# An expert layer and a Mamba scan on one core: LayerNorm moved to the odd body, B copies ahead of evacuations, the last sums side by side, the fourth B product and SiLU one tile later

## The reference

```python
# L0: mixture of experts on every pixel (E = 4 experts, 192 hidden, the best 2 by router)
gates = softmax over the top 2 of (tokens @ router_w.T + router_b), 0 for the others
out   = sum_e gates[e] * (gelu(tokens @ fc1_w[e].T + fc1_b[e]) @ fc2_w[e].T + fc2_b[e])
x     = x + scale * out
# L1: Mamba over the pixels of each image, once forwards and once backwards
x_norm = (x - mean) * rsqrt(var + 1e-5) * gamma + beta          # over the 96 channels
xr, z  = split(x_norm @ W_in)                                   # 192 + 192
xr     = silu(causal_conv4(xr) + conv_b)
dt     = softplus((xr @ W_xproj[:, :6]) @ W_dt + b_dt);  Bm, Cm = xr @ W_xproj[:, 6:]
h_t    = exp(dt_t * A) * h_{t-1} + (dt_t * xr_t) * B_t          # 192 channels x 16 states
y      = (sum over the 16 states of h_t * C_t + xr * D) * silu(z)
out    = 0.5 * (y_forward + y_backward) @ W_out + x
```

## Time and profile before

| | |
|---|---|
| median of three runs | 6058.42 us |
| the profiled execution | 6065.3 us, of which span 6063.5 us |
| TensorE matmul busy | 4967.7 us (82%) |
| VectorE busy | 5276.6 us (87%) |
| ScalarE busy | 4307.0 us (71%) |
| GpSimd busy | 5156.9 us (85%) |
| mean granted TensorE clock | 0.855 of 2.4 GHz |
| DMA | 159 GB/s over the span |

### The profile page before, as it was taken

One profiled execution on the slowest core, in us unless ns is written; L12 is line 12 of the kernel. 1 busy time (PEld: TensorE's weight loads), 2 busy tenths in 40 slices (PEclk: granted clock), 3 DMA queues, 4 the chain that ended last, 5 costly groups with the idle time before them and its releaser, 6 DMA issues.

```text
span 6063.5 us, 68824 instructions
## 1 busy us (share of the span) xinstructions
PE 4967.7 (82%) x14273; PEld 1536.1 (25%) x14273; DVE 5276.6 (87%) x4474; ACT 4307.0 (71%) x6471; POOL 5156.9 (85%) x2127
## 2 busy tenths in 40 slices
PE   7777888878888888888888778887888888888787
PEld 7222222222222222222222222222222222222222
DVE  1239989998999989999899999999899998999998
ACT  0447777777777777777777777777677777777776
POOL 0039989998899998999898998989899998999898
PEclk9878789888888888887898789878888888988898
DMA  3046767676676767676776767666676767766776
GB/s 94 22 98 163 168 164 175 160 174 157 166 173 156 176 155 175 166 171 160 169 173 159 171 160 173 166 163 169 159 175 163 171 161 171 170 165 165 170 172 149
DMA packets 428356, 964.98 MB, mean 159 GB/s; under 512 B 58080, under 2 KB 58329, under 8 KB 394984
## 3 DMA queue, kind: packets, MB, share of 16 engines
q1 hardware_dynamic: 428008, 961.31, 65.6%
HBM read 776.98 MB, written 184.11 MB: 159 GB/s over the span
## 4 chain that ended last, share of the span: by engine, by line
issue 25%; PE 25%; DVE 14%; DMA 10%; POOL 9%; ACT 7%; SPq 2%; DVEq 1%; ACTq 0%; POOLq 0%
DVE X L1163 11%; PE ps L677 8%; POOL X L1250 4%; DMA bc_d<-bc 3%; PE ps L708 3%; POOL X L1240 3%; DMA lo_d<-bc 3%; DMA lo<-lo_d 2%; PE ps L699 2%; PE ps L702 2%; PE ps L656 2%; ACT ps L939 1%; DVE X L1147 1%; PE ps L717 1%; DMA y_d<-yf 1%
## 5 line engine op out<-in xcount | busy, mean ns | idle before, releaser
L1250 POOL TENSOR_TENSOR X<-X,cR 128x2048 f32<-128x2048 f32 x768 | 3479.1, 4530 | 62.0
L1163 DVE TENSOR_TENSOR_SCAN X<-ps,carry,X 128x512 f32<-128x512 f32 x2688 | 3261.6, 1266 | 87.9 <-ACT ps L939 71.3
L939 ACT ACTIVATE ps<-hi,amat 128x512 f32<-128x512 f32 x2048 | 1377.1, 684 | 829.3 <-DVE X L1163 826.1
L1147 DVE TENSOR_TENSOR X<-hi,ps 128x2048 f32<-128x2048 f32 x512 | 1164.6, 2275 | 244.6 <-PE ps L708 133.7
L1240 POOL TENSOR_TENSOR X<-lo,bR 128x2048 f32<-128x2048 f32 x258 | 1168.5, 4529 | 21.8 <-DMA lo<-lo_d 21.8
L708 PE MATMUL ps<-X,red 128*32 128x512 f32 x6144 | 922.9, 676 | 305.6 <-POOL X L1250 304.5
L677 PE MATMUL ps<-win,w_u 97*128 97x512 f32 (+1 forms) x2080 | 1112.7, 684 | 5.9 <-DMA win<-xn_d 4.8
L939 ACT ACTIVATE ps<-lo,amat 128x512 f32<-128x512 f32 x1026 | 688.8, 679 | 163.1 <-DVE X L1163 120.7
L692 PE MATMUL ps<-xr,wd 128*96 128x512 f32 (+1 forms) x520 | 381.6, 826 | 280.4 <-ACT xr L894 227.3
L640 PE MATMUL ps<-xp,w 96*128 96x512 f32 x864 | 524.2, 738 | 54.8 <-DMA xp<-in_x 51.2
L677 PEld LDWEIGHTS ps<-win,w_u 97*128 97x128 f32 (+1 forms) x2080 | 369.7, 188 | 669.5 <-issue 634.5
(11 more groups left out here) (111 smaller groups left out, 4352.1 us busy)
## 6 DMA issues: line engine op xcount, KB each, us to landing
hi<-hi_d SPq DMA_DIRECT2D x516, 512.0 KB, 8.2
bR<-bc_d SPq DMA_DIRECT2D x516, 256.0 KB, 4.6
lo<-lo_d SPq DMA_DIRECT2D x516, 256.0 KB, 4.5
cR<-bc_d SPq DMA_DIRECT2D x516, 256.0 KB, 7.1
hi_d<-S SPq DMA_DIRECT2D x258, 256.0 KB, 8.0
y_d<-yf SPq DMA_DIRECT2D x128, 256.0 KB, 8.8
yb<-y_d SPq DMA_DIRECT2D x128, 256.0 KB, 7.4
win<-xn_d SPq DMA_DIRECT2D x130, 196.3 KB
```

The source lines that it names most:

```text
L939: A_(p_a[i % RING][:, :], dt, ACT.Exp, scale=amat[:, column(i):column(i) + 1]).then_inc(s_exp, 1)
L1147: V.tensor_tensor(X[:, slot(par, s), :, :], hi[:, par, HIGH:2 * HIGH, :], p_b[:, :].unsqueeze(1).to_broadcast([P, BATCH, CH]), ALU.mult).t ...
L1163: V.tensor_tensor_scan(h, a, h, 0.0 if head else carry[:, i:i + 1], ALU.mult, ALU.add).then_inc(s_scan, 1)
L1250: G.tensor_tensor(batch(par, s), batch(par, s), quads(cR, par, s), ALU.mult).then_inc(s_hc, 1)
```

## The change

LayerNorm leaves the even body for the odd one. `ln_mean` heads the odd body's list on TensorE (where `hidden(3)` stood; this goes behind `hidden(5)`), `ln_var` stands behind the last two sums and ahead of `y_begin(1)`; `ln_centred` moves on ScalarE to i = 5, behind the evacuation, `ln_rstd` to i = 8, behind the copy of the output; `normalise` on GpSimd to between the second and the third C product; `store_xn` on SP to the odd body. The operations themselves stay as they are.

On ScalarE in every body, `copy_b` 0 goes from i = 5, behind `evacuate`, to i = 4, and `copy_b` 1 from behind `copy_out` to ahead of it. On TensorE the sums of batches 4 and 5 of the body before stand together behind the third expert product in even bodies, with the other three behind them, and the sum of batch 2 stands ahead of `project(1)` and no longer behind it. The fourth B product on VectorE and SiLU on ScalarE move from i = 19 to i = 20. The bank lists follow.

```diff
--- before.py
+++ after.py
@@ -100,9 +100,9 @@
     out = [("OUT", 1)] if fin else []
     z = [("Z1", 2), ("Z0", 1)] if next_rev else []
     if odd:
-        return (D_BANKS + [("H3", 0)] + out + [("H4", 2), ("H5", 1), ("G3", 2), ("G4", 0), ("U0", 1), ("G5", 2), ("U1", 0)] + z)
-    return (D_BANKS + [("Y2", 0), ("MU", 0)] + out + [("GT", 2), ("VAR", 0), ("H0", 1), ("H1", 2), ("H2", 0),
-                                                       ("G0", 2), ("G1", 0), ("U0", 1), ("G2", 2), ("U1", 0)] + z)
+        return (D_BANKS + [("MU", 0), ("VAR", 0)] + out + [("H4", 2), ("H5", 1), ("H3", 0), ("G3", 2), ("G4", 0), ("U0", 1), ("G5", 2), ("U1", 0)] + z)
+    return (D_BANKS + [("Y2", 0)] + out + [("GT", 2), ("H0", 1), ("H1", 2), ("H2", 0),
+                                           ("G0", 2), ("G1", 0), ("U0", 1), ("G2", 2), ("U1", 0)] + z)
 
 
 def count(uses, bank):
@@ -568,7 +568,7 @@
                 load_high(n + 1, nxt)
                 if fin:
                     store_out(*finished(img, q, rev, odd)[:2], u)
-                if not odd:
+                if odd:
                     store_xn(*piece_before(img, j), pc - 1)
                 if not rev:
                     store_y(1, n, chunk_of(q, rev, odd))
@@ -768,7 +768,7 @@
                 windows = (img * (BODIES // 2) + q + ((NCH // 2) * rev + 2)) * 16
 
                 if odd:
-                    hidden(3, pc, u)
+                    ln_mean(u)
                     sum_states(n - 1, NB - 2, nxt)
                     sum_states(n - 1, NB - 1, nxt)
                 else:
@@ -778,24 +778,22 @@
                         expert_out(m, u, None)
                     if before is not None:
                         sum_states(n - 1, NB - 2, nxt)
-                    expert_out(3, u, None)
-                    expert_out(4, u, None)
-                    if before is not None:
                         sum_states(n - 1, NB - 1, nxt)
-                    expert_out(5, u, None)
+                    for m in range(3, HT):
+                        expert_out(m, u, None)
                     expert_bias(u)
+                if odd:
+                    ln_var(pc - 1, u)
                 y_begin(1, n, f, par)
-                if not odd:
-                    ln_mean(u)
                 if fin:
                     finish(u, n - 1, finished(img, q, rev, odd)[2], nxt)
                 sum_states(n, 0, par)
                 if odd:
                     hidden(4, pc, u)
                     hidden(5, pc, u)
+                    hidden(3, pc, u)
                 else:
                     gates_transposed(nimg, j, u)
-                    ln_var(pc - 1, u)
                     for m in range(3):
                         hidden(m, pc, u)
                 sum_states(n, 1, par)
@@ -806,8 +804,8 @@
                 project(0, par, urev, u)
                 gate_rows(rows + 2, u, even)
                 y_begin(0, n, f, par)
+                sum_states(n, 2, par)
                 project(1, par, urev, u)
-                sum_states(n, 2, par)
                 if nrev:
                     project_z(1, nxt, u)
                     project_z(0, nxt, u)
@@ -984,21 +982,21 @@
                         softplus_start(0, u, n + 1)
                     if i == 3:
                         softplus_log(0, n + 1)
+                    if i == 4:
+                        copy_b(n, 0, par)
                     if i == 5 and before == 0:
                         evacuate(n - 1, 0, img * NCH + (NCH - 1 if rev else q * 2 + odd - 1))
-                    if i == 5:
-                        copy_b(n, 0, par)
                     if i == 6 and not odd:
                         copy_x2(u, pc - 1)
-                    if i == 7 and not odd:
+                    if i == 5 and odd:
                         ln_centred(u, pc - 1)
                     if i == 8:
+                        copy_b(n, 1, par)
                         if before == 1:
                             copy_out(u)
-                        copy_b(n, 1, par)
                     if i == 9 and not odd:
                         copy_gates(u)
-                    if i == 10 and not odd:
+                    if i == 8 and odd:
                         ln_rstd(u, pc - 1)
                     if i == 11:
                         gelu(u, range(3, 6) if odd else range(3))
@@ -1008,7 +1006,7 @@
                         evacuate(n, 1, img * NCH + q * 2 + odd)
                     if i == 16:
                         copy_b(n, 3, par)
-                    if i == 19:
+                    if i == 20:
                         silu_x(u, par)
                         if nrev:
                             silu_z(u, nxt)
@@ -1192,8 +1190,8 @@
                         gate_y(n, True, par)
                     if i in (14, 15, 16):
                         gate_hidden((3 if odd else 0) + i - 14, u)
-                    if i in (7, 11, 15, 19):
-                        times_b(n, i // 4 - 1, par)
+                    if i in (7, 11, 15, 20):
+                        times_b(n, (7, 11, 15, 20).index(i), par)
                     scan(n, i, rev, par, head)
 
             bodies(dve, body)
@@ -1265,10 +1263,10 @@
                 times_c(n, 0, par, rev)
                 times_x(0, u, nxt)
                 times_c(n, 1, par, rev)
+                if odd:
+                    normalise(pc - 1)
                 times_c(n, 2, par, rev)
                 times_b(n + 1, 0, nxt)
-                if not odd:
-                    normalise(pc - 1)
                 times_c(n, 3, par, rev)
                 times_b(n + 1, 1, nxt)
                 times_c(n, 4, par, rev)
```

## The result

The changed kernel takes 6233.97 us (median; 6225.16 to 6243.95), the kernel before, run beside it, 6061.58 (6050.98 to 6075.53): a ratio of 1.029, with a 95% interval of 1.0273 to 1.0306. It is 2.9% slower. The prediction of 6005 us and its range up to 6090 are both wrong. The profiled execution took 6225.16 us, of which span 6223.3, with a mean granted clock of 0.841 (before 0.855).

The account below looks back on a forecast made before the run. VectorE and GpSimd were taken to bound the kernel, with VectorE's idle time to win. Terms: -108 - 74 + 19 + 14 - 12 - 10 + 80 + 38 = -53 us off the 6058.42 median, giving 6005 us; range 5900 to 6090.

Parts of the forecast that it names:

- last sums side by side: TensorE, reverse even body: gated output waits less for the last sum; 0.5 x 24 bodies = -12 us.
- Removed: 107.8 us: VectorE's B products no longer wait for ScalarE's copy of B, which now runs first; 107.8 us counted as won.
- Removed: 133.7 - 60 = 74 us: B products' waits for TensorE's sum go, except 60 us in each image's first reverse body; 74 us counted as won.
- with the product's own wait gone, the even body shows this too: Reverse even body: a scan waits for the exponential behind SiLU, as in the odd one (0.85 us); +14 us (0 to 30).
- it is given back: Rival, 0.18: gated output and evacuation wait for GpSimd instead; 40 us of the gain return, 6045 us or so.
- The even body loses 2.5 us of ScalarE work, two matmul pairs and 1.2 us of GpSimd: LayerNorm leaving the even body shortens scan 15's wait for ScalarE; only forward bodies counted, -10 us.
- SiLU and the product one tile on: End of each body: product directly ahead of its scan, +19 us; later SiLU making the last scans wait, +14 us.
- waits at scans 12 and 15: Odd bodies, LayerNorm's work on ScalarE and TensorE delays exponentials and Gelu: +80 us in reverse, +38 us in forward bodies.
- The waits of the eight first reverse bodies: First reverse body of each image: product still waits for the sum behind TensorE's wait for stored y; 60 us left standing.
- The link of product and scan: VectorE, fourth product directly ahead of the scan reading it: 0.3 us in each of 64 bodies, +19 us (7 to 51).
- the odd body takes it well: Rival, 0.22: TensorE runs at 2.4 GHz when y starts, output no later, 20 us of the 80 and 38 remain; 5907 us.
- The rival on the slower side: Rival, 0.20: odd body queues up on ScalarE at the output's copy, TensorE cold all the way; 6142 us, decided from 6100.

Follow-up runs that it names:

- even filling: Changed kernel plus three zero-weight matmul pairs on TensorE behind the gate transposition of even bodies; 6152.02 us (1.0174).

## Why the prediction was wrong

The runs give a price in time for each part of the change (us by medians; "alone" is the kernel before with that part, "last" the changed kernel against the one without it):

| part | predicted | alone | last |
|---|---|---|---|
| copies of B and third sum | -108 - 74 = -182 | +9 | not run |
| LayerNorm | -10 + 80 + 38 = +108 | +120 | +163 |
| SiLU and fourth product | +19 + 14 = +33 | +57 | +98 |
| last sums side by side | -12 | not run | +3 |
| all | -53 | | +172 |

**The step that failed: a removed wait was counted as time won.** "Removed: 107.8 us" and "Removed: 133.7 - 60 = 74 us" went into the sum in full. With just these two parts the kernel is 9 us slower than before (1.0004 to 1.0036), where 182 us were to be won. That is 191 of the 225 us by which the prediction missed. The waits did go, 224 us of them, but VectorE then met the next limit on its path: the exponentials behind SiLU (+104 us), sums for the gated outputs (+40), and gated hidden and scans 11 and 15 (+73). The prediction had seen this kind of exchange twice. For the eight first reverse bodies it said that SiLU "holds the last scan as long", and counted nothing; elsewhere it wrote that "with the product's own wait gone, the even body shows this too", and gave it 14 us together with SiLU's move. The runs put the move's own share of waits at the last scans at +19 (26 to 45 with SiLU and product alone), and the share of the removed product waits at +104. So the +69 of the ledger isn't the price of SiLU's later place: with SiLU and the product taken back it is +78. The rival "it is given back" had this outcome, but not this cause: TensorE waits for GpSimd 69 us in the changed kernel where it waited 305, and the high gated output of reverse odd bodies, its sign, waits 0 us where it waited 3. It was given back by ScalarE and by dt products at the low clock.

**The second step: "The even body loses 2.5 us of ScalarE work, two matmul pairs and 1.2 us of GpSimd", counted as -10 us.** The relief of ScalarE was larger (-33). But the two pairs of matmuls were priced as nothing on TensorE, and they stood in its gap while the piece of x arrives. Without them TensorE waits 2 to 5 us in most forward even bodies and 1 to 3 in most reverse even ones, and the hidden products behind run at a granted clock of 0.67 in the body shown. This repeats over the runs: in the six kernels that have LayerNorm moved and no even filling, the hidden products of forward even bodies take 4.5 to 5.5 us (medians); with the even filling, or unfilled with LayerNorm in its old place, 2.8. What that costs hangs on how late the piece comes. The ledger's last two lines are 40 us before, 54 with LayerNorm alone, 138 with SiLU and product taken back, 202 in the changed kernel, and 64 there with LayerNorm taken back. Zeros in the place of one pair give 82 us back. So LayerNorm costs 163 us on top of the rest, 55 over its terms, while its 120 us alone are near them, and on the moved copies and sums without the late SiLU and product it costs 75 (6136.22 less 6061.65). The prediction weighed the clock in the odd body alone, where it was low already.

**The term that was mis-sized.** SiLU and the product one tile on: +33, where they cost 57 alone and 98 as the last part, and some 80 us lie between the product alone and both. TensorE waits longer for SiLU's result, 347.0 us for 227.3 ahead of the dt products and 194.1 for 86.7 ahead of z, and runs the dt products at the lower clock into the next body, so that window, B, C and piece come later. The prediction had said that "TensorE's dt products, and with them its queue in the next body, come 1.2 us later", and then priced just ScalarE's exponentials. With the copies, the third sum and the last sums moved but not LayerNorm, the two cost little (6071.42 us, 10 more than copies and sum): most of the 98 needs the late piece and the missing matmuls together. The Trainium skill, "TensorE: Matmul & The Clock Gate", in the section on oscillation in real kernels, advises to arrange the work so that TensorE doesn't wait between bursts. Here filling three such waits gives 182 us of 6234 back.

**What held.** The odd bodies' waits at scans 12 and 15 were 93 and 50 us more for 80 and 38, with their places as forecast. The waits of the eight first reverse bodies, estimated at 60 us, are 59 in the trace of before. They fell to 12 with the earlier sum (17 with copies and sum alone), though they had been left standing, and the last scan of these bodies waits 30 us instead; they last 50.7 us on average for 50.0, so nothing was won, as counted. The link of product and scan: VectorE is idle for 0.21 us between them, where it overlapped the product's end by 0.08; that is the 0.3 us taken, and over bodies 22 us for 19. The Trainium skill, "VectorE: DVE Perf Modes", in the section on the DRAIN one can't avoid, would have it at nothing; the row differs, as it did in the setup. The rival "the odd body takes it well" is out: reverse odd bodies begin y at 1.2 GHz still (2.07 us for its first pair, the median too), and the output's copy comes 1.8 us later, not 0.7.

**The range.** The three costs measured alone add to 186 us, near the whole's 172; so most of the miss isn't in the adding, but in what was added. The rival on the slower side had a cold TensorE, but put it only into odd bodies, and its highest figure of 6142 is 92 us short. Two questions to the trace of before would have helped. What is VectorE's next wait once the product's is gone? The exponential behind SiLU, half a microsecond away. And which matmuls keep TensorE's clock at 0.92 in a forward even body and at 0.96 in a reverse even one (3052.9 to 3098.4), against 0.73 in a forward odd one?

## What to carry to other kernels

Before a matmul is moved out of a stretch, look at what it stands next to: where TensorE would otherwise wait for a DMA, it may be what keeps the clock up for the products behind it, and its removal can cost more than its time. On an engine with little lead over another (two exponentials here), a long block such as SiLU with its table loads needs a long instruction of the other engine beside it: moved without the product it cost 6.9%, with it 0.9%. A later block also delays what TensorE and the DMA queue do at the turn of the body. A wait on the bottleneck is worth no more than the distance to its next wait: before counting it, find the instruction behind it that needs another engine, and when that result was ready. When such waits vanish and the time doesn't fall, see where they came back, and compare the duration of the same matmuls and the granted clock in both traces.

## What was not expected of the hardware

Matmuls that compute nothing can pay: three pairs of zeros ahead of the z and dt products, with copies and third sum in front, make the kernel 1.1% faster than before (5982.81 us, 0.9873 to 0.9906), the fastest here, though TensorE is busy 153 us longer. Without the two moves the same matmuls cost 0.7%. On one DMA queue a small store (64 KB) behind a window's load lands in 8.3 us, ahead of it in 1.6, and what it gains the load of the piece loses. Whether more of TensorE's gaps could be filled with real work was not tried.
